# Routed experts in groups of 512 tokens instead of tiles of 128, turned by VectorE

## The chip, the cores and the metric

The kernel runs on one core of one Trainium2 chip, in one launch. The metric is the time on the device in microseconds; the median of three runs stands for a kernel. The five engines go by the profile's short names: PE (TensorE; PEld its weight loads), DVE (VectorE), ACT (ScalarE), POOL (GpSimd) and SP (SyncE, which here only issues DMAs).

## The reference

x is 8 blocks of 512 tokens of 512 numbers. Two layers are added to it. The first is a matrix for each block, made by a small network from the block's condition. The second, which this change is about, has a shared part and routed experts (8 of them, each token at its top 2):

```python
shared = jax.nn.silu(xf @ w1) * (xf @ w3) @ w2           # 512 -> 1024 -> 512
s = jax.nn.sigmoid((jnp.concatenate([xf, tf], axis=-1) @ router_W).astype(jnp.float32))
sel_scores = s + router_bias
_, topk_idx = jax.lax.top_k(sel_scores, K)               # K = 2
s_sel = jnp.take_along_axis(s, topk_idx, axis=1)
denom = s_sel.sum(axis=1, keepdims=True)
gates = jnp.where(denom > 1e-09, s_sel / (denom + 1e-09), 1.0 / K).astype(x.dtype)
combine = jnp.zeros((N, E), x.dtype).at[jnp.arange(N)[:, None], topk_idx].add(gates)
h = jax.nn.gelu(jnp.einsum('nc,ech->enh', xf, W1e), approximate=False)
y = jnp.einsum('enh,ehc->enc', h, W2e)
routed = jnp.einsum('ne,enc->nc', combine, y)
return ((shared + routed) / (N_SHARED + K)).reshape(Bb, Tt, C)   # added to x
```

The kernel computes y only for the experts that a token has chosen.

## The kernel before, in words

Every product is done in float32r in three matmuls (helper `mm3`): each operand is cut into a high part (a cast by ACT, or by POOL for expert weights) and a low part (a subtraction by DVE, or POOL), and high x high, high x low and low x high are accumulated in PSUM. A matmul has a stationary side of 128 x 128 and a moving side of 512 columns.

The order of the work is written out by hand for each engine, with semaphores. The stages:

1. The first layer (to about 233 us), block by block. It leaves x1 three times: turned for the products (`x1T_d`), in token order (`x1_d`, stored from `x1tok`), and each token's row twice in `xs_d`, at a place in the region of each of its experts. POOL writes those by indirect DMA (L701) from `x1tok`, which ACT fills from PSUM (`keep_tok`, L802).
2. The shared FFN of block 7 (`ffn(S, ...)`, L1676): 8 chunks of the hidden width, each with 24 matmuls up (into `K` and `L` or `Rb`) and 12 down (into `M[0..3]`). For a chunk, ACT does silu (L445), DVE the product (L458), ACT the high part `gTh` (L448), DVE the low part `gTl` (L460); what is in `after` is done behind a chunk. Behind chunk 3, DVE makes the table of the tiles (`tables`, L941): a chain of small steps, each waiting for the last. SP writes it to DRAM and reads it back into one partition (`tab_i`); then each engine reads its numbers from it with `value` and uses them as addresses. SP puts 128 rows of zeros behind each expert's rows (L577) and zeros into the end of `ys_d` (L569).
3. The experts, tile by tile of 128 rows, two tiles in a loop pass (`rpair`). For a tile, SP loads the rows (L588), PE turns them with four transposes (`tx`, L1660), ACT and DVE cut them (L897, L1276); the first product (`mm1`, 12 matmuls into `L`) has the rows as stationary side and the expert's W1 as moving side; ACT applies gelu (L901); PE turns the result (`th`, L1703), ACT and DVE cut it (L905, L1281); the second product (`mm2`, 12 matmuls into `Rb`) follows, DVE evicts it (L1297), SP stores it to `ys_d` (L604). PE's order is mm1(t+1), tx(t+2), mm2(t), th(t+1). The weights are cut by POOL, once for an expert, into one of two halves of `weh` and `wel` (L722 to L728), and PE picks the half by a register.
4. The FFN of blocks 0 to 6 (`fblock`), seven times 288 matmuls, in a loop. Beside it the sum of a block: x1 in token order is loaded into `xres`, DVE adds the shared part from `M` (L1316, frees `M` for the next block) and the two gathered expert rows times their gates (L1324; POOL gathers them from `ys_d`, L752). SP stores `xres` and only then loads the next.

Of the kernel before, what the change touches and what calls it, by code (L numbers as in the profile page):

```python
# [5 lines left out]
ALU = mybir.AluOpType  # L6
ACT = mybir.ActivationFunctionType
F32 = mybir.dt.float32
# [12 lines left out]
ROW, WOFF, WCNT, AROW, FREE, PAD, PAIRS, NACT = range(8)  # L21

def build(nc, x, cond, base, cw1, cb1, cw2, cb2, ln_g, ln_b, rw, rb, w1, w3, w2, w1e, w2e, out):
# [9 lines left out]
    REGION = N + P  # L34
    ROWS = E * REGION + P
    WSL = KC * HE
# [3 lines left out]
    TILES = (N * TOPK + E * (P - 1)) // P  # L40
    PAIRS_MAX = (TILES + 1) // 2
    TAB = -(-(TILES + 5) // 8) * 8
# [21 lines left out]
    xs_d = nc.dram_tensor("xs_d", (ROWS, D), F32, kind="Internal").ap()  # L64
    tab_d = nc.dram_tensor("tab_d", (TAB, 8), I32, kind="Internal").ap()
    ys_d = nc.dram_tensor("ys_d", (PAIRS_MAX * 2 * P, D), F32, kind="Internal").ap()

# [14 lines left out]
    with ExitStack() as ctx:  # L82
# [12 lines left out]
        TX, TH, HP, YP = K[0], K[1], L, Rb  # L95
# [48 lines left out]
        tabi = sb("tabi", [P, 8], I32)  # L144
        tab = sb("tab", [P, 8])
# [23 lines left out]
        tab_i = sb("tab_i", [1, TAB * 8], I32)  # L169
        sb("route_hold", [P, 160])  # L170
# [5 lines left out]
        with ExitStack() as st:  # L176
            xgh = sb("xgh", [P, KC, P], F32R, st)
            xgl = sb("xgl", [P, KC, P], F32R, st)
            hTh = sb("hTh", [P, KC, P], F32R, st)
            hTl = sb("hTl", [P, KC, P], F32R, st)  # L180
            hg = sb("hg", [P, HE], F32, st)
            yo = sb("yo", [P, 2, D], F32, st)
# [4 lines left out]
        with ExitStack() as st:  # L187
# [7 lines left out]
            zz = sb("zz", [P, GT, 32], F32, st)  # L195
        slf = sb("slf", [P, 2, T])
# [26 lines left out]
        with ExitStack() as st:  # L223
            weraw = sb("weraw", [P, WSL], F32, st)
            xr = sb("xr", [P, 2, D], F32, st)
            weh = sb("weh", [P, 2, 2 * WSL], F32R, st)
            wel = sb("wel", [P, 2, 2 * WSL], F32R, st)
        with ExitStack() as st:
            x1raw = sb("x1raw", [P, KC * T], F32, st)
            xres = sb("xres", [P, TT, D], F32, st)  # L230
            yb = sb("yb", [P, TT * TOPK, D], F32, st)
# [62 lines left out]
        scat = [sem(f"scat{i}") for i in range(6)]  # L294
        tabs = sem("tabs")
        dt_ = sem("dt")
        dy = sem("dy")
        pad_out = sem("pad_out")
# [16 lines left out]
        xr_in = [sem(f"xr_in{i}") for i in range(2)]  # L315
        xg_ps = sem("xg_ps")
# [94 lines left out]
        def tiles(eng, pairs, body):  # L411

            body(0)
            with eng.Fori(1, pairs) as j:
                body(j)
# [1344 lines left out]
```

## Time and profile before

| | us |
|---|---|
| median of 3 runs | 1199.97 (1197.99 to 1203.39) |
| the profiled execution | 1202.75 |
| its span in the trace | 1200.9 |
| mean granted TensorE clock | 0.985 of full |

The profile is of one execution; its span begins with the first instruction and ends with the last. Where PE's matmuls overlap, the distance between two starts says what one costs, not its duration. `L1375` is line 1375 of the kernel; L1375 to L1377 are the three matmuls of `mm3`. The buffers' numbers are left out, so that K is either of two banks.

### The profile page before, as it was taken

The page shows a single profiled execution, that of the slowest core. Times are in us where ns is not written, and L with a number is a line of the kernel's source. Part 1 is how long each engine was busy: PE and PEld are TensorE (multiplying, and loading weights), DVE is VectorE, ACT ScalarE, POOL GpSimd, SP SyncE. Part 2 cuts the span into 40 slices and gives each one's busy share as a digit, 9 for nine tenths or more (in the row PEclk, how much of TensorE's full clock was granted, in tenths as well). Part 3 has the DMA queues.
Part 4 walks back from the last instruction along what each step waited for, and adds up shares of the span by engine and source line. Part 5 has one row for each costly group of instructions (what it writes and reads, how often), then busy time and mean ns, then how long its engine had stood idle before and what let it go on. Part 6 is the DMA issues. An engine that isn't in the chain of part 4 may idle for free.

```text
span 1200.9 us, 18241 instructions
## 1 busy us (share of the span) xinstructions
PE 1160.2 (97%) x5762; PEld 935.4 (78%) x5763; DVE 416.4 (35%) x812; ACT 287.8 (24%) x498; POOL 188.1 (16%) x207
## 2 busy tenths in 40 slices
PE   6999898899999999999999998999999999999998
PEld 5666676778788888888888887888888888888887
DVE  4104653535233333333333334233333314233334
ACT  2212453521222222222222222121211112121211
POOL 2002165642510000000000003202020010202020
PEclk8999999899999999999999999999999999999999
DMA  8562589895332222222222224404031130404031
GB/s 309 227 239 95 207 299 347 289 306 162 129 118 83 79 87 79 79 87 79 82 84 83 83 79 123 175 1 175 1 100 74 39 136 0 175 0 175 0 125 49
DMA packets 70480, 151.82 MB, mean 126 GB/s; under 512 B 9753, under 2 KB 18457, under 8 KB 68658
## 3 DMA queue, kind: packets, MB, share of 16 engines
q1 hardware_dynamic: 57666, 111.55, 26.9%
q0 software_dynamic: 12784, 39.86, 9.4%
q8 instruction: 20, 0.33, 0.1%
q14 instruction: 10, 0.08, 0.0%
HBM read 88.73 MB, written 62.65 MB: 126 GB/s over the span
## 4 chain that ended last, share of the span: by engine, by line
PE 91%; DVE 4%; DMA 2%; POOL 1%; issue 1%; ACT 1%; SPq 0%; DVEq 0%; ACTq 0%
PE L L1375 7%; PE L L1377 7%; PE L L1376 7%; PE Rb L1377 7%; PE Rb L1375 7%; PE Rb L1376 7%; PE M L1375 5%; PE M L1376 5%; PE M L1377 5%; PE K L1376 5%; PE K L1375 5%; PE K L1377 5%; PE Rb L1465 3%; PE K L1703 2%; PE K L1660 2%; PE M L1403 2%
## 5 line engine op out<-in xcount | busy, mean ns | idle before, releaser
L752 POOL DMA_INDIRECT yb<-ys_d,pos_fix x64 | 61.2, 957 | 326.6 <-DVE xres L1324 308.6
L1375 PE MATMUL L<-weh,xgh 128*128 x260 | 107.6, 414 | 1.8 <-issue 1.8
L1276 DVE TENSOR_TENSOR xgl<-K,xgh 128x512 fp32r<-128x512 f32 x66 | 45.7, 692 | 173.4 <-ACT xgh L897 173.4
L1375 PE MATMUL Rb<-weh,hTh 128*128 x256 | 105.5, 412 | 0.0
L1375 PE MATMUL K<-x1h,w13h 128*128 128x512 f32 x256 | 101.6, 397 | 3.0 <-DVE x1l L1355 3.0
L1375 PE MATMUL M<-w2h,gTh 128*128 128x512 f32 x256 | 102.3, 399 | 2.3 <-DVE gTl L460 2.3
L1377 PE MATMUL L<-weh,xgl 128*128 x260 | 102.7, 395 | 0.0
L1376 PE MATMUL L<-wel,xgh 128*128 x260 | 102.5, 394 | 0.0
L1376 PE MATMUL K<-x1l,w13h 128*128 128x512 f32 x256 | 102.0, 398 | 0.0
L1376 PE MATMUL M<-w2l,gTh 128*128 128x512 f32 x256 | 101.9, 398 | 0.0
L1377 PE MATMUL M<-w2h,gTl 128*128 128x512 f32 x256 | 101.8, 398 | 0.0
L1377 PE MATMUL K<-x1h,w13l 128*128 128x512 f32 x256 | 101.7, 397 | 0.0
L1377 PE MATMUL Rb<-weh,hTl 128*128 x256 | 100.5, 393 | 0.0
L1376 PE MATMUL Rb<-wel,hTh 128*128 x256 | 100.2, 391 | 0.0
L445 ACT ACTIVATE slf<-K 128x512 f32<-128x512 f32 x64 | 38.3, 599 | 238.3 <-PE K L1377 234.2
L448 ACT CAST gTh<-slf 128x512 fp32r<-128x512 f32 x64 | 39.7, 621 | 191.7 <-DVE slf L458 191.7
L458 DVE TENSOR_TENSOR slf<-L,slf 128x512 f32<-128x512 f32 x32 | 22.1, 692 | 169.2 <-PE L L1377 162.5
L905 ACT CAST hTh<-K 128x512 fp32r<-128x512 f32 x65 | 38.2, 587 | 163.9 <-PE K L1703 163.9
L1297 DVE COPY yo<-Rb 128x512 f32<-128x512 f32 x64 | 44.3, 692 | 92.2 <-PE Rb L1377 92.2
L701 POOL DMA_INDIRECT xs_d<-x1tok,pos_int x64 | 68.2, 1065 | 38.0 <-issue 24.6
L901 ACT ACTIVATE hg<-L 128x512 f32<-128x512 f32 x65 | 38.9, 598 | 146.5 <-PE L L1377 146.5
L746 POOL COPY pos_fix<-ypos 128x8 int32 (+1 forms) x8 | 2.3, 283 | 442.6 <-DMA ys_d<-yo 390.0
(238 smaller groups left out, 2146.1 us busy)
## 6 DMA issues: line engine op xcount, KB each, us to landing
xr<-xs_d SPq DMA_DIRECT2D x68, 256.0 KB, 2.6
w2c<-in_L_cond_w_dram SPq DMA_DIRECT2D x8, 2048.0 KB, 8.5
ys_d<-yo SPq DMA_DIRECT2D x64, 256.0 KB, 2.1
xtok<-in_x_dram SPq DMA_DIRECT2D x32, 256.0 KB, 7.4
x_d<-x1tok SPq DMA_DIRECT2D x8, 1024.0 KB, 7.9
xres<-x_d SPq DMA_DIRECT2D x8, 1024.0 KB, 9.5
x1T_d<-xp SPq DMA_DIRECT2D x7, 1024.0 KB, 4.6
out_dram<-xres SPq DMA_DIRECT2D x7, 1024.0 KB, 4.8
```

Of the source, the lines that this page charges most:

```text
L445: nc.scalar.activation(slf[:, h % 2], U[h % 2][:], ACT.Silu).then_inc(ffn.silu, 1)
L448: nc.scalar.copy(gTh[:, h % 2], slf[:, h % 2]).then_inc(ffn.g_hi, 1)
L701: pool.indirect_dma_start(out=xs_d, out_offset=bass.IndirectOffsetOnAxis(ap=pos_int[:, c:c + 1].bitcast(U32), axis=0), in_=x1tok[i][:, t, ...
L752: pool.indirect_dma_start(out=yb[:, c, :], out_offset=None, in_=ys_d, in_offset=bass.IndirectOffsetOnAxis(ap=pos_fix[:, c:c + 1].bitcast(U ...
L901: nc.scalar.activation(hg[:], HP[:], ACT.Gelu).then_inc(h_g, 1)
L905: nc.scalar.copy(hTh[:].rearrange("p k n -> p (k n)"), TH[:]).then_inc(ht_hi, 1)
L1276: tt(xgl[:].rearrange("p k n -> p (k n)"), TX[:], xgh[:].rearrange("p k n -> p (k n)").bitcast(F32), ALU.subtract).then_inc(xg_lo, 1)
L1297: nc.vector.tensor_copy(yo[:, s], YP[:]).then_inc(y_sb, 1)
L1375: mm(o, ah, bh_, start=start, stop=False)
L1376: mm(o, ah, bl_, start=False, stop=False)
L1377: return mm(o, al, bh_, start=False, stop=stop)
L1465: last_mm = mm(Rb[32 * q:32 * q + 32, cc * P:(cc + 1) * P], hTz[:, k, 2 * j + part], w[:, k, 2 * q + j], start=(n == 0 and j == 0 and k == 0),
```

## The change

The experts are worked in groups of 512 rows instead of tiles of 128. A region of `xs_d` now ends in 512 rows of padding, the table has 4 columns instead of 8 (`ROW`, `EROW`, `PAD`, `LAST`), and a group knows its expert's rows in W1e and W2e.

- For each group the whole weights are loaded by SP (`load_e1`, `load_e2`), even if the expert is that of the last group, and cut by ACT and DVE in four pieces each. POOL cuts no weights.
- The rows come by four DMAs that place them so that 32 x 32 blocks turned by DVE (`turn_rows`) give x turned; the columns of `x1tok`, `x1_d` and `xs_d` are permuted for that, and DVE undoes it in the first sum of each tile (`fused`, four instructions instead of one).
- The first product has W1 as stationary side and the 512 tokens as moving side, so h comes out turned; no transpose by PE is left in this stage. The second goes chunk by chunk of h over all four token tiles, into the four banks `G`.
- ACT evicts y into `yo`, SP stores it in two halves. The sum goes into `total` instead of into `xres`.
- The zeros: 8 DMAs of 512 rows into `xs_d` from SP, ahead of the load of the first weights, and 7 of 512 rows into `ys_d` from POOL after it.
- x1 of block 0 is loaded and cut in the last group, between evictions.

The core of the diff:

```diff
+        G = K + V
+            sp.wait_ge(tab_in, 16)
+            pad_src = zeros[:].unsqueeze(1).broadcast_to([P, GR * D // (P * P), P])
             with sp.Fori(0, E) as e:
-                row = value(sp, PAD, e, E * REGION - P)
-                sp.dma_start(zero_rows(row), zero_src).then_inc(pad_out, 16)
+                row = value(sp, PAD, e, E * REGION - GR)
+                sp.dma_start(xs_d[ds(row, GR), :].rearrange("(p r) (k c) -> p (r k) c", p=P, c=P), pad_src).then_inc(pad_out, 16)
...
+            def load_rows(g):
+                row = value(sp, ROW, g, E * REGION - GR)
+                rows = xs_d[ds(row, GR), :].rearrange("(n t) (j f) -> j t n f", t=32, j=4)
+                for j in range(4):
+                    sp.dma_start(xr[32 * j:32 * j + 32].rearrange("p t i f -> p (t i) f"), rows[j]).then_inc(xr_in, 16)
...
+            load_e1(0)
+            sp.wait_ge(pad_out, 16 * E)
+            load_rows(0)
+            load_e2(0)
+
+            def load_group(g, n):
+                if n is not None:
+                    sp.wait_ge(e1_lo, n * KC)
+                    load_e1(n)
+                    sp.wait_ge(xt_f, n * TT)
+                    load_rows(n)
+                    sp.wait_ge(e2_lo, n * KC)
+                    load_e2(n)
...
+                sp.wait_ge(ys_zero, 16 * (GROUPS_MAX - SURE))
+                store_y(g, 0)
+                store_y(g, 1)
...
+            pool.wait_ge(e1_in, 16)
+            for g in range(SURE, GROUPS_MAX):
+                pool.dma_start(ys_d[g * GR:(g + 1) * GR, :].rearrange("(p r) (k c) -> p (r k) c", p=P, c=P), zero_src
+                               ).then_inc(ys_zero, 16)
...
+            after[HC - 2] = lambda: [cut_e1(0, m) for m in range(KC)]      # ACT, and the same on DVE
+            ffn_act(act, S, 0, True, after)
+            act.sem_inc(y_sb, Y_FREE)
+            for t in range(TT):
+                cut_x(0, t)
+            def pass_group(g, n):                                          # ACT
+                cut_e2(g, 0)
+                cut_e2(g, 1)
+                gelu(g, 0)
+                cut_e2(g, 2)
+                gelu(g, 1)
+                cut_e2(g, 3)
+                if n is not None:
+                    cut_e1(n, 0)
+                gelu(g, 2)
+                if n is not None:
+                    cut_e1(n, 1)
+                gelu(g, 3)
+                if n is not None:
+                    cut_x(n, 0)
+                    cut_e1(n, 2)
+                    cut_x(n, 1)
+                    cut_e1(n, 3)
+                    cut_x(n, 2)
+                    cut_x(n, 3)
+                keep_y(g, 0)
+                keep_y(g, 1)
+                if n is None:
+                    act.wait_ge(x1raw_in, 16)
+                    act.wait_ge(h_ps, g * KC + KC)
+                    cut_x1(0)
+                keep_y(g, 2)
+                keep_y(g, 3)
...
+            def turn_rows(g, t):
+                dve.wait_ge(xr_in, g * 64 + 64)
+                if not (first(g) and t < 2):
+                    dve.wait_ge(xg_lo, g * TT + (t - 1))
+                nc.vector.transpose(xt[:, t % 2].rearrange("p c (i n) -> p i c n", i=4),
+                                    xr[:, t].rearrange("p i (c f) -> p i c f", c=KC)).then_inc(xt_f, 1)
+            def pass_group(g, n):                                          # DVE
+                cut_e2(g, 0)
+                cut_e2(g, 1)
+                cut_h(g, 0)
+                cut_e2(g, 2)
+                cut_h(g, 1)
+                cut_e2(g, 3)
+                if n is not None:
+                    turn_rows(n, 0)
+                    cut_e1(n, 0)
+                cut_h(g, 2)
+                if n is not None:
+                    turn_rows(n, 1)
+                    cut_e1(n, 1)
+                cut_h(g, 3)
+                if n is not None:
+                    cut_x(n, 0)
+                    cut_e1(n, 2)
+                    turn_rows(n, 2)
+                    cut_x(n, 1)
+                    cut_e1(n, 3)
+                    turn_rows(n, 3)
+                    cut_x(n, 2)
+                    cut_x(n, 3)
...
+            def mm1(g):
+                pe.wait_ge(xg_lo, g * TT + TT)
+                for m in range(KC):
+                    pe.wait_ge(e1_lo, g * KC + m + 1)
+                    pe.wait_ge(y_sb, g * TT + (m - TT + 1 + Y_FREE))
+                    cols = slice(m * P, (m + 1) * P)
+                    for k in range(KC):
+                        last_mm = mm3(G[m][:], e1h[:, k, cols], e1l[:, k, cols], x1h[:, k], x1l[:, k], k == 0, k == KC - 1)
+                    last_mm.then_inc(h_ps, 1)
+
+            def mm2(g):
+                for m in range(KC):
+                    pe.wait_ge(ht_lo, g * KC + (m + 1 + H_FREE))
+                    pe.wait_ge(e2_lo, g * KC + m + 1)
+                    for t in range(TT):
+                        if m == 0:
+                            pe.wait_ge(h_g, g * KC + t + 1)
+                        rows = slice(t * P, (t + 1) * P)
+                        last_mm = mm3(G[t][:], hTh[:, m, rows], hTl[:, m, rows], e2h[:, m], e2l[:, m], m == 0, m == KC - 1)
+                        if m == KC - 1:
+                            last_mm.then_inc(y_ps, 1)
```

## Rows read from the trace of the kernel before

**Rows 1.** The page's busy times: us (share of the span) x instructions:

```profile
PE 1160.2 (97%) x5762; PEld 935.4 (78%) x5763; DVE 416.4 (35%) x812; ACT 287.8 (24%) x498; POOL 188.1 (16%) x207
```

**Rows 2.** Busy time by stage: us, each engine's busy (x), PEclk, DMA share, GB/s:

```profile
233.60:305.50 71.90, 69.60 (x294) 55.44 (x293) 33.05 (x90) 19.24 (x28) 33.44 (x26) 0.98 0.71 236
305.50:311.80 6.30, 4.22 (x22) 3.17 (x21) 1.38 (x2) 1.66 (x3) 2.52 (x2) 1.00 0.31 95
311.80:722.14 410.34, 410.34 (x2047) 340.03 (x2048) 131.45 (x191) 105.77 (x191) 14.33 (x6) 1.00 0.26 88
722.14:725.50 3.36, 0.37 (x4) 0.13 (x3) 2.16 (x4) 2.04 (x4) 0.00 (x0) 1.00 0.29 103
725.50:1197.40 471.90, 471.87 (x2016) 379.24 (x2016) 156.03 (x242) 82.83 (x139) 63.48 (x72) 1.00 0.24 82
726.00:728.80 2.80, 2.80 (x8) 2.22 (x7) 1.29 (x3) 1.50 (x2) 1.62 (x3) 0.50 0.87 311
```

**Rows 3.** Chain of waits, 700 to 740 us: start, us, what:

```profile
702.91 0.44 PE K L1703 x4
725.53 0.58 PE K L1375
726.53 0.43 PE K L1377
```

**Rows 4.** Groups by form: count | busy us, mean ns | idle before:

```profile
L1375 PE MATMUL L<-weh,xgh 128*128 x260 | 107.6, 414 | 1.8 <-issue 1.8
L1375 PE MATMUL Rb<-weh,hTh 128*128 x256 | 105.5, 412 | 0.0
L1660 PE MATMUL K<-ident,xr 128*128 128x128 f32 x264 | 39.4, 271 | 0.0
L1703 PE MATMUL K<-ident,hg 128*128 128x128 f32 x260 | 38.9, 272 | 0.3 <-ACT hg L901 0.3
```

**Rows 5.** Timeline of PE in the experts: start, us, engine, line:

```profile
403.25 0.39 PE L1376 MATMUL L<-wel,xgh 128*128 x1
405.77 0.60 PE L1660 MATMUL K<-ident,xr 128*128 128x128 f32 x4
```

**Rows 6.** Timeline of PE in an FFN block:

```profile
799.95 0.40 PE L1375 MATMUL K<-x1h,w13h 128*128 128x512 f32 x1
805.55 0.40 PE L1375 MATMUL M<-w2h,gTh 128*128 128x512 f32 x1
```

**Rows 7.** Timeline of DVE and SP's queue, and one window of zero writes:

```profile
267.80 0.16 DVE L956 SCALAR_TENSOR_TENSOR tw<-iota,taken 128x8 f32<-128x8 f32 x1
274.87 0.35 SPq L571 DMA_DIRECT2D tab_d<-tabi  x1
278.78 14.04 SPq L577 DMA_DIRECT2D xs_d<-zeros  x8
268.00:269.00 1.00, 1.00 (x6) 0.82 (x5) 0.86 (x5) 0.00 (x0) 0.00 (x0) 1.00 1.00 288
```

**Rows 8.** DMA issues: count, KB each, median us from issue to landing:

```profile
weraw<-in_L_cond_W1e_dram POOLq DMA_DIRECT2D x2, 1024.0 KB, 6.0
x1raw<-x1T_d SPq DMA_DIRECT2D x6, 1024.0 KB, 12.7
```

**Rows 9.** Groups by form of DVE and ACT, columns as in group 4:

```profile
L1165 DVE STREAM_TRANSPOSE zz<-L 32x128 f32<-32x128 f32 x32 | 10.0, 313 | 0.6
L1276 DVE TENSOR_TENSOR xgl<-K,xgh 128x512 fp32r<-128x512 f32 x66 | 45.7, 692 | 173.4 <-ACT xgh L897 173.4
L934 ACT CAST x1h<-x1raw 128x512 fp32r<-128x512 f32 x28 | 15.2, 615 | 0.9 <-DVE hTl L1281 0.9
```

**Rows 10.** Timelines of ACT and DVE at two places:

```profile
296.54 0.60 ACT L445 ACTIVATE slf<-K 128x512 f32<-128x512 f32 x1 [4.16 <-PE K L1377]
300.79 1.99 DVE L460 TENSOR_TENSOR gTl<-slf,gTh 128x512 fp32r<-128x512 f32 x1 [0.69 <-ACT gTh L448]
800.22 0.69 DVE L458 TENSOR_TENSOR slf<-L,slf 128x512 f32<-128x512 f32 x1 [3.93 <-PE L L1377]
```

More of the change, by code:

```diff
@@ L408, in value, with groups @@
             alone(eng)
-            return eng.value_load(tab_i[0:1, ds(at_ * 8 + col, 1)], min_val=lo, max_val=hi)
[L411 to L415, printed above, removed]
+            return eng.value_load(tab_i[0:1, ds(at_ * COLS + col, 1)], min_val=lo, max_val=hi)
+        H_FREE, Y_FREE, YO_FREE = 2, KC, 16
+        def groups(eng, body):
+            last = value(eng, LAST, 0, GROUPS_MAX - 1, 1)
+            with eng.Fori(0, last) as g:
+                body(g, g + 1)
+            body(last, None)
+            return last
         def alone(eng):
@@ new lines, in keep_y, with cut_x1 @@
+            def keep_y(g, t):
+                act.wait_ge(y_ps, g * TT + (t + 1 + Y_FREE))
+                act.wait_ge(y_out[t // 2], g * 16 + YO_FREE)
+                nc.scalar.copy(yo[:, t], G[t][:]).then_inc(y_sb, 1)
+            def cut_x1(b):
+                for c in range(KC):
+                    nc.scalar.copy(x1h[:, c], x1raw[:, c * T:(c + 1) * T]).then_inc(xf_hi, 1)
+            after = {h: lambda h=h: cut_piece(UP_PIECES + 1 + h) for h in range(PIECES - UP_PIECES - 1)}
+            after[HC - 2] = lambda: [cut_e1(0, m) for m in range(KC)]
@@ L1306, in prepare, with fused @@
                 dve.wait_ge(xres_in, m * 16 + 16)
+                if not first(m):
+                    dve.wait_ge(out_st, m * 16)
+            def fused(t, part, scale, n, done_):
+                if n is not None:
+                    dve.wait_ge(acc, n)
+                    ins = nc.vector.scalar_tensor_tensor(out=total[:, t], in0=part, scalar=scale, in1=total[:, t],
+                                                         op0=ALU.mult, op1=ALU.add)
+                else:
+                    for j in range(4):
+                        ins = nc.vector.scalar_tensor_tensor(
+                            out=total[:, t].rearrange("p (c j f) -> p j c f", j=4, c=KC)[:, j],
+                            in0=part.rearrange("p (c j f) -> p j c f", j=4, c=KC)[:, j], scalar=scale,
+                            in1=xres[:, t].rearrange("p (j c f) -> p j c f", j=4, c=KC)[:, j],
+                            op0=ALU.mult, op1=ALU.add)
+                ins.then_inc(done_, 1)
             def add_shared(t, of, n, done_):
@@ L1726, in fblock, with pass_group, banks_f @@
+            pe.sem_inc(y_ps, Y_FREE)
+            pe.wait_ge(tab_in, 16)
+            pe.wait_ge(S.silu, HC)
+            pe.wait_ge(S.g_f, HC)
+            def pass_group(g, n):
+                mm1(g)
+                mm2(g)
+            last = groups(pe, pass_group)
+            def banks_f(h, i):
+                t = G.index((U, V)[i][h])
+                pe.wait_ge(y_sb, last * TT + (t + 1 + Y_FREE))
             def fblock(b):
-                ffn(F, b, (lambda h, i: None) if first(b) else None, lambda k: pe.wait_ge(xf_lo, b * KC + k + 1),
+                ffn(F, b, banks_f if first(b) else None, lambda k: pe.wait_ge(xf_lo, b * KC + k + 1),
```

395 lines of the change are left out of this document (145 added, 250 removed).

## The prediction

> **What bounds the kernel now.** First the page's busy shares [rows 1]: TensorE is busy for 97% of the span, no other engine over 35%. So a change pays only where it takes work from TensorE, or where TensorE stands still. Then the table by stage [rows 2]: the experts run from 305.50 to 722.14 us (416.6 us), with TensorE without a gap from 311.80; ahead of them is a start with some 2 us idle, behind them 3.4 us of which it works 0.4, then 471.9 us of seven FFN blocks, 67.41 each. The chain of waits [rows 3] shows what fills the experts: matmuls, and between them groups of four transposes at 0.44 us a group; and at the change of stage a restart in which matmuls take 0.43 us each instead of some 0.23, the granted clock being 0.50, the lower level (1.2 GHz) [rows 2], after an idle of 3 us. Eight or so such matmuls cost 1.6 us.
>
> How many tiles: the first expert product has 65 x 4 matmuls of each of its three kinds, the second 64 x 4 [rows 4]. And W1e is loaded from DRAM only twice [rows 8], once for an expert that has rows: two experts are in use. 4096 tokens, each at two different experts, in 64 tiles of 128: both have 4096 rows, 32 full tiles. In groups of 512 that is 16 full groups, none padded, and one expert's weights serve eight groups.
>
> **The matmuls.** Before, 64 tiles x 24 = 1536 matmuls of 512 columns; after, 16 x (48 + 48) = 1536. The same number (the extra 65th first product, 2.7 us, goes). Between 403.25 and 405.77 lie 11 dynamically addressed matmuls, 0.2291 each [rows 5]; between 799.95 and 805.55 lie 24 of the FFN with fixed addresses, 0.2333 each [rows 6]. After the change every operand of the experts has a fixed address and the form of the FFN (128 columns cut from a 512-wide tile against a whole 512 chunk). I take 0.2333: 1536 x 0.2333 = 358.4 us. The other end, 0.2291, gives 351.9. 
>
> **The transposes.** 264 + 260 of them [rows 4], 131 groups at 0.44 = 57.6 us, all on TensorE's path. They go: rows of x come by DMA as 32-partition bands and VectorE turns them in 32x32 blocks, and h comes out turned since the weights are now the stationary side. A tile was 24 x 0.2291 + 2 x 0.44 = 6.38 us, which times 64 is 408.6; the new 22.4 us a group times 16 is 358.4.
>
> **What ACT and DVE get for it, per group of 22.4 us.** ACT: 4 casts each of e2, e1, x and h, 4 gelus, 4 evictions of y: 24 at 0.615 at most [rows 9] = 14.8. DVE: 16 subtractions at 0.69 [rows 9] = 11.0, and four turns of 128x512. A turn of 32x128 takes 0.313 [rows 9]; for 512 elements the ends are 0.313 and 4 x 0.313 = 1.25; I take 0.75, near the 0.69 of the other 512-element operations. 14.0 together. Both fit, so order and arrival count:
> - First product 0 to 11.2 us of the group, its four chunks at 2.8 apiece; second 11.2 to 22.4, y chunks ready at 20.3, 21.0, 21.7, 22.4.
> - ACT: casts of e2 from 0.7, gelu(0) at 2.9, gelu(1) 5.7, gelu(2) 8.5, gelu(3) 11.3 to 11.9. The second product's first chunk overwrites the bank of tile 3 at 13.3: 1.4 us to spare.
> - SP is in order: store y (0.8), load e1 of the next group, its rows (four DMAs), e2. A loop pass with a table read and an issue takes SP 14.04 / 8 = 1.8 us [rows 7]. e1 is issued at 2.6 and lands at 8.6 (6.0 for 1 MB [rows 8]), wanted from 7.6; the rows come behind it, 1 MB at 288 GB/s [rows 7] = 3.6 us: 12.2.
> - From there DVE works off four turns, four subtractions of e1, two of h, four of x: 4 x 0.75 + 10 x 0.62 (back to back) = 9.2, ending at 21.4. The next group needs all of x at 22.4. One us of slack, the tightest place of the steady state.
> Loop overhead: an FFN block takes 67.41 against 288 x 0.2333 = 67.19, so 0.2 a pass, 15 passes: 3.0 us.
>
> **The start, where the change pays.** The padding of xs_d grows from 9 x 256 KB to 8 x 1 MB = 8.39 MB, and now stands in SP's queue ahead of the load of e1; ACT and DVE cut e1 ahead of the last chunk of the shared FFN, and x rows wait for all padding. The table is made in 16 short linked steps instead of 33 from 267.80 (0.21 each): the store goes out at 271.2, not 274.87; padding starts 3.9 later, as before (274.87 to 278.78) [rows 7], at 275.1, data from 277. Zero writes alone ran at 288 GB/s with the DMA engines full [rows 7]: 29.1 us, to 306.2. e1 behind it: cast possible from 310.2. ACT then casts e1 (2.4), and only then does silu(7), at 312.7 instead of 296.54 [rows 10]; slf(7), gTh(7), gTl(7) follow, and TensorE's last chunk of the shared FFN, which could have started at 302, starts at 315.6: 13.6 us idle. It ends at 320.0, slow restart included. The rows of group 0 have landed at some 313.4; DVE's four turns and four subtractions from 315.5 end at 320.9. First expert matmul at 321.0 instead of 305.50 (first product of tile 0). What gets better here: POOL no longer cuts weights, beside which gTl(7) took 1.99 instead of 0.69 [rows 10].
> Bounds of this start: with padding at twice the speed (landed by 292) nothing waits but x itself, and TensorE starts the experts at 307; with padding at half the speed, 350.
> POOL writes another 7.3 MB of zeros into ys_d from 311, and SP waits for these ahead of the first store of y, with the load of e1(2) queued behind. All that is to move after 306 (7.3 MB of zeros, 2.1 of rows, 3.1 of weights) takes 41 us, to 347, while the first store of y is due at 343: the rows of group 2 are late by some 3 us against a slack of 1, part of which the queue makes good. I put 1.5 us, once (0 to 6).
>
> The Trainium skill (DMA: Bandwidth & Descriptors, Queues, rings and completion order) says that each DMA engine goes round between the queues that have work, packet by packet. The trace has no place to show it for a zero write beside a load. By it e2(0), e1(1) and the rows of group 1 get half the engines each time, and the latter land at 334 instead of 320; DVE would then cut h(2) at 336, wanted at 338. It changes no term, but eats the cover.
>
> **The end.** Before: last tile, cast of h, x1 cut after it, restart at half clock, 725.53 [rows 3]. Now x1 of block 0 is loaded in group 15 and cut between evictions of y, at 21.7 of the group: first k at 23.0, 0.7 us gap, no 3 us idle. Gain against before: 2.7 of gap, 1.6 of restart.
> **The FFN blocks.** Adding into a total splits each first sum in four (16 x 0.31 at most instead of 4 x 0.62: 2.5 us more for DVE ahead of the block's first slf, before which it stands idle for 3.93 [rows 10]): nothing; in the last block it sits before slf(7), 0.7 us. Casts of x1tok in a permuted order: same number of elements, nothing.
>
> **The sum.** 321.0 + 358.4 + 3.0 + 1.5 + 0.7 = 684.6, where block 0 starts now at 725.53. Then 1200.9 - 725.53 - 1.6 + 0.7 = 474.5. Span 1159.1 against 1200.9: 41.8 us less. The profiled execution took 1202.75, 1.85 over its span; so 1161 on its scale. The median shown is 1199.97; less 41.8 that is 1158. I predict 1159.
>
> **Rivals.**
> - Matmuls at 0.2291 as in the old experts: 1152. For: it was so in this stage for 400 us. Against: all fixed-address stages show 0.2333.
> - Rows of the next group late, or the turn at 1.25 us: 1 to 2 us idle in each of 15 groups, 1174 to 1189. For: the slack is 1 us by my own count, built from bounds. Against: SP's time of 1.8 for a pass is from a DMA-bound stretch.
> - Padding slower than 288 GB/s, at half: 29 us more at the start, 1188. Against: 288 was measured in three windows of 1 us on end, one of which is shown.
> - Slower than before: the loads of a group take what x1raw takes in the FFN blocks, 12.7 us [rows 8]. e1 then lands at 15.3, gelu(2) stalls the second product, rows land near 19, x is ready at 28, 5.6 us late; with 1.6 for the restart at the lower clock 7 a group, 108 in all: 1266. It decides where the stall passes 41.8 / 15 = 2.8 us a group. Against: those loads run beside the gathers of yb, which the experts don't have.
> - It doesn't do what it says: more than 16 groups, if experts were more than two. Excluded by the two loads.
>
> **Chances.** Forecast 0.54, the matmul rate 0.16, late rows or slow turns 0.17, slow padding 0.08, slower loads 0.04, anything near no change 0.01. The likeliest one's own range is 1153 to 1168; with the matmul rate below, and most of the late rows above, 1148 to 1182. Faster by over 0.5% (what can be told from no change here) 0.95, same 0.01, slower 0.04.
>
> **What would show it.** No transposes between 320 and 684; TensorE's idle of 12 to 15 us around 302 to 316, ended by DVE's gTl, with ACT waiting on the e1 DMA; then some 22.4 to 22.6 us a group at full granted clock; spacing 0.2333; block 0 a us after the last y. Wrong: a regular gap at each group's start ended by DVE's x1l (late rows), a turn near 1.25, no idle at 302, or groups at 22.0.

## The result, and the profile after

The changed kernel takes 1181.8 us in the median of 4 runs (1181.18 to 1184.73), against 1200.96 for the kernel before in 4 runs (1197.99 to 1203.39; three of them are those of the first table): a ratio of 0.9846, 95% interval 0.9818 to 0.9875. A second time, with 5 runs beside 17 of before, it was 1180.94 and 0.9863 (0.9842 to 0.9883). So it is faster, by some 19 us (1.5%), where 42 were forecast. 1181.8 lies just inside the end of the range, and only since errors of opposite sign met, as shown below. The profiled execution took 1181.49, its span is 1179.5.

The page's busy shares (us, share of the span, instructions) already say that something stands in the way:

```profile
PE 1096.6 (93%) x5226; PEld 878.3 (74%) x5226; DVE 482.2 (41%) x1015; ACT 393.8 (33%) x687; POOL 164.3 (14%) x200
```

TensorE was at 97% [rows 1]; now its work is 64 us less and 83 us of the span are idle. The table by stage (columns as in rows 2) places the idle. The stages are: shared FFN, its last chunk with the wait for x, group 0, group 1, groups 2 to 15, FFN blocks; then two short windows used below.

```profile
233.60:309.48 75.88, 58.73 (x254) 47.00 (x252) 25.21 (x65) 15.70 (x24) 21.13 (x21) 0.93 0.80 241
309.48:315.72 6.24, 4.42 (x12) 3.25 (x13) 5.26 (x8) 3.40 (x5) 3.16 (x3) 0.76 1.04 395
315.72:352.84 37.12, 26.20 (x96) 20.94 (x97) 12.45 (x20) 13.69 (x25) 0.00 (x0) 0.77 0.77 238
352.84:377.55 24.71, 22.21 (x97) 17.78 (x96) 12.45 (x20) 13.17 (x25) 0.00 (x0) 1.00 0.61 170
377.55:710.36 332.81, 312.45 (x1344) 250.16 (x1345) 167.97 (x270) 184.28 (x332) 0.00 (x0) 1.00 0.63 174
710.36:1179.50 469.14, 465.58 (x2016) 378.52 (x2016) 163.76 (x339) 83.79 (x141) 62.53 (x72) 1.00 0.24 85
337.00:343.00 6.00, 0.00 (x0) 0.00 (x0) 0.12 (x1) 0.00 (x0) 0.00 (x0) 0.50 1.01 179
386.00:391.00 5.00, 5.00 (x23) 4.13 (x23) 0.00 (x0) 3.38 (x6) 0.00 (x0) 1.00 1.24 197
```

Groups 2 to 15 take 332.81 / 14 = 23.77 us each, where 22.6 were forecast; group 0 takes 37.12; the FFN blocks 469.14 instead of 474.5. TensorE's waits of the whole kernel, the three longest (engine, tile and line that waited, then whose release came last: us in total, times, longest):

```profile
PE M L1445 <- DVE gTl L475: 17.5, 3, 14.5
PE K L1445 <- ACT yo L930: 17.3, 14, 1.3
PE K L1445 <- DVE hTl L1318: 15.4, 8, 10.9
```

The first is the start that was forecast. The second comes 14 times, once for each of groups 2 to 15: a regular gap. The third is one stall of 10.9 in group 0 and seven small ones. VectorE's own waits say what is behind the last two (count | busy us, mean ns | idle before, and what ended it). Under it stand rows of the first and of the second expert product:

```profile
L1298 DVE STREAM_TRANSPOSE xt<-xr 128x512 f32<-128x512 f32 x64 | 45.0, 705 | 111.2 <-DMA xr<-xs_d 111.0
L1445 PE MATMUL K<-x1h,e1h 128*128 128x512 f32 x128 | 51.7, 404 | 19.1 <-ACT yo L930 17.3 <-DVE x1l L1304 1.8
L1445 PE MATMUL K<-e2h,hTh 128*128 128x512 f32 x128 | 52.1, 407 | 15.8 <-DVE hTl L1318 15.4
```

VectorE stood idle for 111.0 us before its turns, waiting for rows of x: 7 us a group. A turn takes 705 ns.

**One group, read closely.** The timeline from 377.55, where TensorE starts a group (start, us, engine, line, idle before):

```profile
377.80 1.38 SPq L613 DMA_DIRECT2D ys_d<-yo  x2
381.08 0.40 SPq L597 DMA_DIRECT2D e1raw<-in_L_cond_W1e_dram  x1
382.41 2.02 SPq L608 DMA_DIRECT2D xr<-xs_d  x4
392.20 0.71 DVE L1298 STREAM_TRANSPOSE xt<-xr 128x512 f32<-128x512 f32 x1 [6.33 <-DMA xr<-xs_d]
398.80 0.71 DVE L1298 STREAM_TRANSPOSE xt<-xr 128x512 f32<-128x512 f32 x1
399.49 0.39 PE L1447 MATMUL Rb<-e2h,hTl 128*128 128x512 f32 x1
399.54 0.62 ACT L917 CAST x1h<-xt 128x512 fp32r<-128x512 f32 x1 [1.18 <-DVE xt L1298]
400.07 1.07 ACT L930 COPY yo<-K 128x512 f32<-128x512 f32 x2
401.13 0.47 PE L1445 MATMUL K<-x1h,e1h 128*128 128x512 f32 x1 [1.25 <-ACT yo L930]
```

SP issues e1 at 3.5 us of the group (2.6 forecast), since both stores of y stand ahead of it in its queue, each waiting for ScalarE's evictions. The rows follow at 4.9 and are there at 14.65 (12.2 forecast), not 3.6 but 5.6 us behind e1: the window 386 to 391 above, in which the rows travel and e2 is issued behind them, shows 197 GB/s at a DMA share of 1.24, not the 288 of the zero writes [rows 7]. The last turn starts at 21.25, the cast of it follows, and only behind this cast in ScalarE's order come the evictions of y that free the banks. TensorE has finished at 399.7 and starts at 401.13. The profile names ScalarE's eviction; but that eviction, and the last subtraction of x as well, stand behind VectorE's turn, and the turns behind the rows. Experiments 1 and 2 test that.

**Group 0** shows the same thing larger:

```profile
315.13 10.37 SPq L608 DMA_DIRECT2D xr<-xs_d  x4
342.88 0.71 DVE L1298 STREAM_TRANSPOSE xt<-xr 128x512 f32<-128x512 f32 x1 [17.25 <-DMA xr<-xs_d]
344.82 0.79 PE L1445 MATMUL K<-e2h,hTh 128*128 128x512 f32 x1 [10.92 <-DVE hTl L1318]
```

The rows of group 1 are wanted while POOL's 7.3 MB of zeros are under way: four DMA issues keep SP for 10.4 us, the rows are there 27.7 us after the first of them, and VectorE, which stands at the first turn, has the cut of h(2) queued behind it. So TensorE stops in the middle of the second product, and restarts on the lower level of the clock (0.50 in the window 337 to 343; behind 344.82 a matmul takes 0.43 us, as in rows 3).

### The profile page after: what moved, and what is told of

It reads as the page before. It is cut to its first block, busy times and chain, and to the rows that moved or that the text cites. A ratio compares the mean times of both kernels' runs of the same rounds, so it can differ in the third digit from the quotient of the medians.

```text
span 1179.5 us, 15385 instructions
## 1 busy us (share of the span) xinstructions
PE 1096.6 (93%) x5226; PEld 878.3 (74%) x5226; DVE 482.2 (41%) x1015; ACT 393.8 (33%) x687; POOL 164.3 (14%) x200
## 4 chain that ended last, share of the span: by engine, by line
PE 55%; DMA 15%; DVE 12%; SPq 7%; issue 7%; ACT 2%; POOL 1%; ACTq 0%; DVEq 0%; POOLq 0%
DMA xr<-xs_d 12%; PE K L1445 5%; PE K L1447 5%; PE K L1446 5%; PE M L1445 4%; PE M L1446 4%; PE M L1447 4%; SPq L419 3%; DVE xt L1298 3%; PE Rb L1535 3%; PE L L1447 2%; PE L L1446 2%; PE L L1445 2%; PE Rb L1447 2%; PE Rb L1446 2%
## 5 line engine op out<-in xcount | busy, mean ns | idle before, releaser
L1298 DVE STREAM_TRANSPOSE xt<-xr 128x512 f32<-128x512 f32 x64 | 45.0, 705 | 111.2 <-DMA xr<-xs_d 111.0
L917 ACT CAST x1h<-xt 128x512 fp32r<-128x512 f32 x64 | 39.7, 621 | 115.3 <-DVE xt L1298 115.3
L728 POOL DMA_INDIRECT xs_d<-x1tok,pos_int x64 | 67.2, 1050 | 34.4 <-issue 18.6
L1445 PEld LDWEIGHTS M<-w2h,gTh 128*128 128x128 f32 x256 | 48.5, 189 | 30.3 <-DVE gTl L475 18.8
L1445 PE MATMUL K<-x1h,e1h 128*128 128x512 f32 x128 | 51.7, 404 | 19.1 <-ACT yo L930 17.3
L473 DVE TENSOR_TENSOR slf<-Rb,slf 128x512 f32<-128x512 f32 x32 | 22.1, 691 | 114.0 <-PE Rb L1447 114.0
L1445 PE MATMUL K<-e2h,hTh 128*128 128x512 f32 x128 | 52.1, 407 | 15.8 <-DVE hTl L1318 15.4
L1318 DVE TENSOR_TENSOR hTl<-hg,hTh 128x512 fp32r<-128x512 f32 x64 | 43.9, 686 | 52.2 <-ACT hTh L925 52.2
L475 DVE TENSOR_TENSOR gTl<-slf,gTh 128x512 fp32r<-128x512 f32 x64 | 44.3, 692 | 47.5 <-ACT gTh L463 47.5
L1473 PE MATMUL M<-xTh,bh 128*128 128x512 f32 x128 | 56.2, 439 | 6.0 <-DVE bl L1129 3.2
L1447 PEld LDWEIGHTS M<-w2h,gTl 128*128 128x128 f32 x256 | 48.4, 189 | 11.7
```

The source lines that it names most:

```text
L473: nc.vector.tensor_tensor(slf[:, h % 2], V[h % 2][:], slf[:, h % 2], ALU.mult).then_inc(ffn.g_f, 1)
L475: nc.vector.tensor_tensor(gTl[:, h % 2], slf[:, h % 2], gTh[:, h % 2].bitcast(F32), ALU.subtract).then_inc(ffn.g_lo, 1)
L728: pool.indirect_dma_start(out=xs_d, out_offset=bass.IndirectOffsetOnAxis(ap=pos_int[:, c:c + 1].bitcast(U32), axis=0), in_=x1tok[i][:, t, ...
L917: nc.scalar.copy(x1h[:, :, t * P:(t + 1) * P], xt[:, t % 2]).then_inc(xg_hi, 1)
L1298: nc.vector.transpose(xt[:, t % 2].rearrange("p c (i n) -> p i c n", i=4), xr[:, t].rearrange("p i (c f) -> p i c f", c=KC)).then_inc(xt_f, 1)
L1318: tt(hTl[:, m], hg[:, m % 2], hTh[:, m].bitcast(F32), ALU.subtract).then_inc(ht_lo, 1)
```

## The experiments

Experiments 1 to 4 were run side by side, so were 5 to 8, and so were the second run of 1 with 9 and 10; 11 had only the kernel before beside it. Up to the store of the tables an execution can take up to 22 us longer than in the changed kernel's first profile; for the kernel before it is 7 to 9 us (experiment 10). It isn't the chip alone: experiments 1 to 4 and 5 to 8 ran on the same one, and the kernel before took 1212.49 beside the first four and 1198.35 beside the others. What moves this stage is not known. So what an edit does is read from the stages behind that store, and times are compared within one such set of runs.

**1. Stores of y from ScalarE's queue.** Edit, in SP's and in ScalarE's order of work:

```diff
-                store_y(g, 0)      # SP, at the end of load_group
-                store_y(g, 1)
+                store_y(g, 0)      # ScalarE, behind keep_y(g, 1)
+                store_y(g, 1)      # ScalarE, behind keep_y(g, 3)
```

The wait for the zeros in `ys_d` goes with the stores.

> The stores of y are issued from ACT's queue behind its evictions, so that SP doesn't wait for them ahead of the next group's loads; all else as in the changed kernel. Theory A (the groups wait for the rows of the next one, which land 14.6 us into a group because SP issues their loads only after the last store of y): SP issues e1 some 5 us earlier, the rows land near 9.5, the gap of 1.4 us at each group's start is gone; 1181.8 less 14 x 1.4 = about 1162. Rival B (what comes last is the serial work of DVE and ACT on a group, whatever the arrival): the gap stays, 1180 to 1184.

Measured: 1176.26 (1169.26 to 1181.19), ratio to before 0.9683 (0.9602 to 0.9764), tables stored at 286.06 instead of 264.30. It was run a second time beside experiment 9, in which the changed kernel's own stages are unaltered:

> The stores of y from ScalarE's queue once more, on a chip where the tables of the changed kernel come at 264 and not at 286. Theory A (the late rows of groups 2 to 15 are their whole excess): 14 x 2.0 us less than the changed kernel's 1180.9, 1153 to 1156, all groups from 1 on at 21.76. Theory B (its 1176 of the first run was no accident of the chip): 1170 or more.

Measured: 1169.19 (1167.81 to 1175.06), ratio 0.9675 (0.9634 to 0.9716), against 1197.94 for the kernel of experiment 9: 28.8 us less, where 14 x 2.0 = 28 were expected. The tables came at 279.61 here and at 278.48 there, so the expectation's condition of tables at 264 wasn't met, and its absolute figure isn't tested. The windows of group 0, of groups 1 to 15, and of one group, and VectorE's turns with their wait for rows:

```profile
332.46:368.80 36.34, 24.48 (x97) 19.69 (x97) 12.45 (x20) 13.22 (x24) 0.00 (x0) 0.81 0.80 245
368.80:695.20 326.40, 326.40 (x1441) 270.17 (x1439) 180.67 (x288) 199.41 (x352) 0.00 (x0) 1.00 0.66 189
390.56:412.32 21.76, 21.76 (x98) 18.02 (x96) 12.45 (x20) 13.58 (x24) 0.00 (x0) 1.00 0.66 215
L1298 DVE STREAM_TRANSPOSE xt<-xr 128x512 f32<-128x512 f32 x64 | 44.9, 703 | 23.2 <-DMA xr<-xs_d 23.0
```

PE busy equals the window: 326.40 / 15 = 21.76 a group without one gap, in both runs. VectorE's wait for rows falls from 111.0 us to 23.0, of which 18.2 is the stall of group 0, which stays. 21.76 / 96 is 0.2267 us a matmul, below both ends that I had taken. So the regular gap goes when the two stores no longer stand in front of the loads, and theory A holds. Stage by stage, the two profiles differ by 27.9: groups 2 to 15 with the turn to block 0 take 306.3 instead of 334.5 (28.2 less), group 1 takes 1.7 less, and all else together is 2.0 longer. The absolute expectations (1162; 1153 to 1156) were missed, as the early stage was 15 to 22 us longer than in the first profile.

**2. Rows as 2 KB pieces.** The rows load unsplit, four DMAs of 128 whole rows. This kernel leaves out the order of x that the turns need, so it serves for the time alone. Two things change at once: the size of a piece, and the partitions that a DMA fills, 128 instead of 32.

```diff
-                rows = xs_d[ds(row, GR), :].rearrange("(n t) (j f) -> j t n f", t=32, j=4)
+                rows = xs_d[ds(row, GR), :].rearrange("(j p) d -> j p d", p=P)
                 for j in range(4):
-                    sp.dma_start(xr[32 * j:32 * j + 32].rearrange("p t i f -> p (t i) f"), rows[j]).then_inc(xr_in, 16)
+                    sp.dma_start(xr[:, j].rearrange("p i f -> p (i f)"), rows[j]).then_inc(xr_in, 16)
```

> The rows of a group are read as whole rows of 2 KB instead of four pieces of 512 B each; x then stands in another order, so what is turned isn't the x of the reference, all times of the engines being the same. Theory A with the size of the piece as its cause (1 MB of rows at some 190 GB/s, 5.6 us, where whole rows of weights come at some 380): rows land 2.8 us earlier, gap gone, and group 0 gains as well: 1155 to 1162. If the order in SP's queue alone makes them late: rows still land past 13 us, 1175 or more. Rival B: 1180 to 1184.

Measured: 1158.86 (1155.01 to 1163.42), ratio 0.9536 (0.9466 to 0.9606). In one group, which starts at 493.17:

```profile
496.42 0.40 SPq L597 DMA_DIRECT2D e1raw<-in_L_cond_W1e_dram  x1
504.75 0.71 DVE L1298 STREAM_TRANSPOSE xt<-xr 128x512 f32<-128x512 f32 x1 [3.35 <-DMA xr<-xs_d]
```

SP's order is unchanged and e1 goes out at 3.25, yet the first turn is at 11.6, 3.1 earlier than in the changed kernel, and every group from 1 on takes 21.76. Between 498.0 and 503.5 the DMA engines moved 352 GB/s at a share of 0.98, against 261 at 1.16 in the like stretch of the changed kernel (383.5 to 392). Group 0 lasts 28.35, its stall is 3.4. So the form of the rows' DMAs is a second cause; whether it is the size of a piece or the 32 partitions isn't separated. Either cure alone removes the gap of groups 2 to 15: the two delays add up on one chain, whose excess is 2 us a group.

**3. Padding of 128 rows.**

```diff
-                sp.dma_start(xs_d[ds(row, GR), :]..., pad_src).then_inc(pad_out, 16)
+                sp.dma_start(xs_d[ds(row, P), :].rearrange("p (k c) -> p k c", c=P), pad_src[:, 0:KC]).then_inc(pad_out, 16)
```

> Padding of xs_d is 128 rows an expert instead of 512 (here no row of it is ever read, all groups being full): 2.1 MB instead of 8.4 ahead of the first weights. Theory: TensorE's idle from 294.9 to 309.5 goes, first expert matmul at about 302 instead of 315.7 (-14), and since POOL's zeros into ys_d then start at 280 and not at 304, the stall of 11.3 us in group 0 goes too (-13): about 1155. Rival (the stall in group 0 comes from the loads' own size): only -14, about 1168.

Measured: 1184.41 (1180.16 to 1189.47), ratio 0.9766 (0.9689 to 0.9843), tables at 279.85. SP's padding and TensorE's two waits of the start:

```profile
284.81 14.91 SPq L586 DMA_DIRECT2D xs_d<-zeros  x8
312.62 0.51 PE L1445 MATMUL M<-w2h,gTh 128*128 128x512 f32 x1 [2.10 <-DVE gTl L475]
318.92 0.77 PE L1445 MATMUL K<-x1h,e1h 128*128 128x512 f32 x1 [3.24 <-DVE x1l L1304]
```

14.91 instead of 24.91 for a quarter of the bytes, at a DMA share of 0.42: what is left is SP's loop, 1.86 a pass. From the store of the tables to the first expert matmul it is 39.1 us, 51.4 in the changed kernel: 12.3 saved, 14 expected. The stall of group 0 stays, 11.0, as the rival had it; but POOL's zeros went out only at 307.70, behind the load of e1, and not at 280, so this experiment doesn't tell whether the zeros cause it. The next one does.

**4. Zeros into ys_d early.** POOL issues the seven zero writes ahead of its wait for XW (66.26 us) instead of at 304.56.

```diff
+            pool.wait_ge(cond_ps, 4)
+            for g in range(SURE, GROUPS_MAX):
+                pool.dma_start(ys_d[g * GR:(g + 1) * GR, :]..., zero_src).then_inc(ys_zero, 16)
             pool.wait_ge(xw_hi, 1)
...
-            pool.wait_ge(e1_in, 16)
```

> The 7 MB of zeros into ys_d are issued by POOL near 65 us, where the DMA engines are half busy, instead of at 304. Theory: the idle at 295 to 309 stays, the stall of 11.3 us in group 0 and its restart go: about 1168. Rival (the rows of group 1 are late by the loads alone): 1178 or more. If the early zeros delay the loads of the first stage, that stage is longer by up to 5 us.

Measured: 1188.18 (1185.15 to 1189.68), ratio 0.9792 (0.9722 to 0.9862), tables at 279.42. Groups 0 and 1:

```profile
331.25:353.09 21.84, 21.84 (x97) 18.09 (x97) 12.55 (x20) 13.51 (x25) 0.00 (x0) 1.00 0.42 97
353.09:376.58 23.49, 22.25 (x97) 17.78 (x96) 12.46 (x20) 13.07 (x25) 0.00 (x0) 1.00 0.67 179
```

45.3 instead of 61.8: 16.5 less, and no stall. The later groups keep their gap. So the stall was these zeros. The time itself gives 1188 where 1168 was expected: the tables came 15 us later than in the first profile, and the FFN blocks were at the longer of their two lengths (experiment 9).

**5 and 6. The changed and the first kernel again,** on one chip, as controls.

> The changed kernel once more, as the control for the others on this chip. Groups 2 to 15 at 23.8 us each with an idle of 1.25 ahead of each, group 0 with a stall of 11 us: these come from the kernel and return. The store of the tables was at 264.3 us in its first profile and at 279 to 286 in the four experiments run on another chip. Theory A: this early stage is bound by transfers and moves with chip and execution, so it is at 270 to 286 here, and the ratio to the kernel before stays at 0.98 to 0.99 since that one has the same stage. Theory B: the 6.9 us by which the early stage was shorter than before's (274.87 less the 3.7 of the shorter table) is the change's: the store stays within 2 us of 264.

> The kernel before, with a profile on the same chip. By A its tables are stored as much later than 274.87 as the changed kernel's are later than 264.3, within 5 us; by B the difference between the two is again 10 to 11 us, and more than the 3.7 of the shorter table in every pair. The FFN blocks: 67.4 us each as before if the length belongs to the program; the changed kernel had 67.0 in two profiles and 67.4 in three, so I expect it to vary by some 0.4 with no cause in the code.

Measured: 1180.94 (1179.16 to 1183.76), ratio 0.9863; and 1197.33 (1194.49 to 1202.58), ratio 0.9994 (0.9976 to 1.0013). The stores of the tables, before and after:

```profile
273.33 0.35 SPq L571 DMA_DIRECT2D tab_d<-tabi  x1
```

```profile
263.34 0.32 SPq L577 DMA_DIRECT2D tab_d<-tabi  x1
```

10.0 us between them, as 10.6 the first time. In other sets the changed kernel's store moves by more than that (A), but here the difference stays 6.3 above the 3.7 of the shorter table (B). All of the changed kernel's gaps return: an idle of 1.25 ahead of 14 groups, 12.1 in group 0.

**7 and 8. The three edits together, and the tables earlier.** Experiments 1, 3 and 4 in one kernel; then besides it

```diff
-            after[3] = lambda: tables(dve)
+            piece1 = after[1]
+            after[1] = lambda: [piece1(), tables(dve)]
...
+            after[HC - 2] = lambda: [[cut_e1(0, m) for m in range(KC)], dve.wait_ge(tab_in, 16),
+                                     turn_rows(0, 0), turn_rows(0, 1)]
...
-            dve.wait_ge(tab_in, 16)
-            turn_rows(0, 0)
-            turn_rows(0, 1)
```

> Stores of y from ScalarE's queue, zeros into ys_d written at some 65 us, padding of 128 rows, together. Theory A (three separate waits, each with its own cause): tables to first expert matmul 39 us as with the short padding alone (51.4 in the changed kernel), group 0 without its stall, all 16 groups at 21.76: 280 + 39 + 348 + 2 to block 0, 470 behind it, 1139 of span, 1141 in time; ratio to the changed kernel 0.952 to 0.962. Theory B (the rows' 512-byte pieces at some 188 GB/s are the bound, and what one edit frees another takes): 5 to 20 us above that, with DVE waiting for rows in most groups.

> The same with the tables made after chunk 1 of the shared FFN instead of chunk 3, and the first two turns of group 0 ahead of VectorE's last chunk. Theory A: tables are stored 15 us earlier, padding, e1 and rows of group 0 are there before the shared FFN ends, TensorE never waits at 302 and for 1 to 3 us ahead of the first expert matmul: 5 us less than with the three edits alone, 1136. Theory B: VectorE then waits for rows inside its chunk 7 or the tables' data come late, and it is the same or 3 us more.

Measured, beside the two controls: 1123.55 (1120.26 to 1127.02), ratio to before 0.9374 (0.9355 to 0.9394), and 1120.58 (1113.35 to 1121.36), ratio 0.9339 (0.9313 to 0.9364). Against the changed kernel's 1180.94 that is 57.4 and 60.4 less. The first one's windows from the last shared chunk on (that chunk and the wait for x, group 0, groups 1 to 15):

```profile
294.67:301.83 7.16, 3.06 (x12) 2.20 (x13) 5.26 (x8) 3.40 (x5) 0.00 (x0) 1.00 0.77 269
301.83:325.30 23.47, 23.47 (x97) 19.23 (x97) 12.54 (x20) 13.03 (x24) 0.00 (x0) 0.93 0.51 139
325.30:651.70 326.40, 326.40 (x1441) 270.09 (x1439) 180.83 (x288) 199.32 (x352) 0.00 (x0) 1.00 0.67 186
```

The single gains add up: 28.8 (stores) + 12.3 (padding) + 16.5 (zeros) = 57.6, against 57.4. That they agree to 0.2 is luck: the changed kernel's groups 2 to 15 alone took 332.8 and 336.0 in two profiles. From the store of the tables to block 0 the kernel of the three edits is 57.8 us shorter than the changed kernel beside it, and its FFN blocks are 2.5 longer in all. All groups from 1 on are at 21.76, so nothing that one edit freed was taken by another, and theory A holds; the ratio to the changed kernel is 0.951, where 0.952 to 0.962 was expected. The absolute times lie 15 to 18 us under the expectation, since the tables came at 262.74 and 250.60 and not at 280 and 265. Of the second, the start and all sixteen groups:

```profile
297.87 0.47 PE L1444 MATMUL K<-x1h,e1h 128*128 128x512 f32 x1 [1.02 <-DVE x1l L1304]
```

```profile
297.87:646.03 348.16, 348.16 (x1536) 288.18 (x1536) 193.38 (x308) 212.51 (x376) 0.00 (x0) 1.00 0.67 184
```

The experts are 1536 matmuls without a gap, and start 4.0 us earlier (5 expected); the times alone (intervals that overlap) would not show that. The tables were stored 12.1 us earlier, but from there to the experts it takes 47.3 us instead of 39.1: all but 1.0 of the two waits of the start is gone, and TensorE has no more to gain there. This one is the fastest kernel of the study.

**9. Where TensorE's program lies.** Five semaphore increments on TensorE's queue ahead of the shared FFN.

```diff
+            for _ in range(5):
+                pe.sem_inc(spare, 1)
```

> The changed kernel with five semaphore increments more on TensorE's queue ahead of the shared FFN, which do nothing else. An FFN block took 67.20 us in both profiles of before, 66.44 in three (the changed kernel twice, the short padding) and 66.7 to 66.8 on the mean in the others, to 0.02 the same within each kernel, while TensorE's instructions and its operands' places are the same in all but before. Theory A: the length hangs on where TensorE's loop lies in the program, which every other edit shifts too: blocks of some other length, 66.6 to 67.3, here. Theory B: it comes from the work on the other queues (it was the edits to stores and zeros that changed it): 66.44 again. Groups 2 to 15 at 23.8 and 1181 to 1186 by both.

Measured: 1197.94 (1193.01 to 1201.88), ratio 0.9892 (0.9857 to 0.9927), tables at 278.48. One FFN block each (us, busy) of the kernel before, of the changed one, of experiment 7, and of this one:

```profile
794.36:861.56 67.20, 67.20 (x290) 54.03 (x289) 21.29 (x34) 11.84 (x20) 7.77 (x9) 1.00 0.22 79
```

```profile
776.88:843.32 66.44, 66.44 (x289) 54.10 (x288) 22.04 (x46) 11.84 (x20) 7.80 (x9) 1.00 0.22 79
```

```profile
720.13:787.05 66.92, 66.92 (x290) 54.20 (x289) 22.05 (x47) 11.84 (x20) 7.78 (x9) 1.00 0.22 79
```

```profile
791.21:857.65 66.44, 66.44 (x290) 54.10 (x288) 22.05 (x47) 11.84 (x20) 7.78 (x9) 1.00 0.22 79
```

66.44 is what theory B expected, but B falls as well: the kernel of experiment 1 had 66.8 in its first profile and 66.44 in its second, with not a byte changed. The length varies from one execution to another, 66.44 or 66.8 to 66.9, in kernels after; in three profiles of kernels before (experiment 10 among them) it was 67.2. What sets it stays open.

**10. The regions of xs_d.** The kernel before with `REGION = N + 4 * P` instead of `N + P`, as after.

> The kernel before with 4608 rows of xs_d to an expert instead of 4224, as the changed kernel has it, and nothing else. Its tables were stored at 274.87 and 273.33, the changed kernel's at 264.30 and 263.34; 3.7 of the 10.3 is the shorter table. Theory A: the other 6.6 comes from where the scatter writes its rows in DRAM: store at 267 to 269 here, and 4 to 7 us less in time. Theory B: from something else (the place of the program, the zeros written to ys_d at 255 us): store at 273 to 275, time as before.

Measured: 1212.47 (1208.39 to 1219.44), ratio 1.0019 (0.9995 to 1.0043), tables at 281.88, where those of experiment 9's kernel beside it came at 278.48. The place of the rows in DRAM gains nothing in time. In this set the difference between the two kernels is 3.4, the shorter table and no more; so the 6.3 to 6.9 of the sets with early tables isn't a fixed property of the change either.

**11. Full padding with the early tables.** Experiment 8 with 512 rows of padding again.

> The kernel of the early tables with the full padding back (512 rows to an expert), for the question whether the 10 us of it matter once the tables come early. From the store of the tables it takes 4.6 to the first padding, 24.9 for the padding, 3.4 and 8.1 to e1 in SBUF, 41.0 in all, and rows of group 0 some 2 us later. With the early tables that store was 45.9 us ahead of TensorE's last chunk of the shared FFN having its operand (296.5 at its end less 250.6). Theory A: e1 lands 2 to 5 us ahead of the need and the first expert matmul is 3 to 6 us later than with the short padding: 1123 to 1127 on a chip with tables at 250, a ratio to the kernel before of 0.937 to 0.941. Theory B: the padding's queue holds back the last pieces of the shared weights, which are still being loaded at 250, and silu(7) waits again: 10 us or more, 0.945 or above.

Measured: 1154.65 (1153.0 to 1155.96), ratio 0.9499 (0.9471 to 0.9528), tables at 271.86. The stretch from the store of the tables to their coming back, the wait for e1, and TensorE's wait that follows from it:

```profile
271.86:277.40 5.54, 5.54 (x25) 4.52 (x25) 0.74 (x2) 0.63 (x2) 1.92 (x2) 1.00 1.03 407
316.88 2.18 ACT L895 CAST e1h<-e1raw 128x512 fp32r<-128x512 f32 x4 [11.95 <-DMA e1raw<-in_L_cond_W1e_dram]
326.02 0.79 PE L1444 MATMUL M<-w2h,gTh 128*128 128x512 f32 x1 [11.38 <-DVE gTl L475]
```

Theory A failed. The numbers are those of B (10 us or more, 0.945 or above), its mechanism is not: e1 landed 45.0 us after the store, not 41.0, because from the store to the first padding it took 8.4 us, not 4.6. The tables now travel while the DMA engines are full (share 1.03) with the store of x1 and POOL's last scatters. Experiment 8 had shown it (250.60 to 258.82), and I left it out. TensorE reached its wait 42.8 us behind the store, so e1 was late for silu(7), which stands behind the cast of e1, as in the changed kernel. From tables to experts it is 59.4 us, 47.3 with the short padding: 12.2, as in experiment 3 (12.3). The difference of the two ratios, 0.016 or 19 us, is larger; the rest lies ahead of the store of the tables, before the padding is written, where sets differ without a known cause.

## Why the prediction was wrong, point by point

| | forecast | measured | difference |
|---|---|---|---|
| store of the tables | 271.2 | 264.30 | -6.9 |
| from there to the first expert matmul | 49.8 | 51.4 | +1.6 |
| groups 0 and 1 | 46.7 | 61.8 | +15.1 |
| groups 2 to 15 and the turn to block 0 | 316.9 | 332.8 | +15.9 |
| FFN blocks | 474.5 | 469.1 | -5.4 |
| span | 1159.1 | 1179.5 | +20.4 |

- **Number of groups, no transposes, work per group:** right. 16 groups of 96 matmuls. ACT works 184.28 / 14 = 13.2 and DVE 12.0 a group, 14.8 and 14.0 were put.
- **Matmul rate:** 0.2333 was taken, with 0.2291 as the other end; it is 0.2267 in the experts (experiments 1, 2, 7, 8), and a pass of the loop costs nothing to be seen. That is 10.2 + 3.0 = 13.2 us too dear, which hid a part of the other error. Going by likeness to the FFN's form was no ground: neither form predicted the rate. The Trainium skill (TensorE: Matmul & The Clock Gate, Wait — 56ns, not 53.3ns?) has 2.5 ns over N / 2.4 GHz, so 215.8 ns; even the best stretch lies 11 ns above it.
- **The failed step: "One us of slack, the tightest place of the steady state", from e1 "issued at 2.6", "1 MB at 288 GB/s" and "22.4 us".** Measured: e1 issued at 3.5 and landed at 9.1 (+0.5 against 8.6), rows 5.6 behind it (+2.0 against 3.6), so at 14.65 for 12.2; VectorE's chain 8.7 instead of 9.2; and the group is to last 21.76, not 22.4. So x is ready at 23.35 where it was wanted at 21.76. What this costs is 332.8 - 14 x 21.76 - 0.7 = 27.5 us over groups 2 to 15; 28.2 came back there, against experiment 9's kernel, when the stores left SP's queue (experiment 1). The table shows only 15.9 for them, since the matmul rate and the passes gave 12 back: so the time stayed inside the range by luck. The rate of the rows was the weakest term: 288 GB/s was read off writes of a constant tile and used for reads in 512-byte pieces.
- The Trainium skill (DMA: Bandwidth & Descriptors, Specifications) puts the full rate at 512 bytes and above. These runs differ, as far as experiment 2 tells: 512-byte reads of xr into 32 partitions gave 261 GB/s together with e1, 2 KB ones into 128 partitions 352.
- **The rival "rows of the next group late"** was this mechanism, priced at 1 to 2 a group and 1174 to 1189; 2.0 a group and 1181.8 were measured. It was held for less likely than the forecast, 0.17 against 0.54; the slack of 1 us was built from three terms each uncertain by 1, and should have had the larger share.
- **Zeros into ys_d, the second step that failed:** 1.5 (0 to 6) was put, 15.3 in group 0 and 1.2 in group 1 is what they cost (experiment 4 gives back 16.5). The sum behind the 1.5 has a slip too: 12.5 MB at 288 GB/s is 43 us, not 41. I let the rows of group 2 be late, against the first store. They were late for group 1 already, since the zeros were under way at the same time; the prediction's paragraph on the sharing between queues had named this (rows at 334). It changed "no term" there only because the rows of group 1 were held to be wanted after h(2); in VectorE's order the turn stands ahead of it, and they landed at 342.8.
- **The start:** an idle of 13.6 forecast, 14.5 measured, at the forecast place and with ACT waiting 19.04 us for e1. Zero writes ran at 284 GB/s from 271 to 293. Experiment 3 shows that 12 us from the tables to the experts are the size of the padding; that SP's loop makes the rest wasn't tested.
- **The end:** 0.7 us gap forecast, 0.66 idle measured at 710.36, and no restart at the lower clock.
- **The transposes:** 64 tiles of 6.38 us are 408.2, not 408.6; nothing hangs on it.
- **FFN blocks:** "nothing" was wrong by 5.3: 66.44 a block against 67.20. **Tables:** 6.9 earlier than 271.2. Neither was in the forecast as anything but zero, both came in its favour, and neither is explained (experiments 9 and 10 excluded a cause each).

## What to carry to other kernels

In a loop where one queue both stores results and loads the next inputs, every load waits for the last result: put the stores on another queue before counting on any slack (here 28.8 us of 1198). The wait that the profile names for it can be two engines away from the cause, so follow it back through what each engine has queued. A transfer's rate is to be taken from a transfer of the same direction and piece size, and fill-in writes of zeros belong where the DMA engines have room (here near 66 us), since an engine that waits for one late load holds back all that is queued behind it. When the slack in a steady loop is smaller than the sum of the errors of its terms, take the late case for the likelier one; it is paid in every pass.

## What the runs showed that I had not expected

- Matmuls of 512 columns, at the full granted clock and without a wait, start 0.2267 us apart in the experts and 66.44 / 288 = 0.2307 or 67.20 / 288 = 0.2333 apart in FFN blocks; the same program showed 66.44 and 66.8 in two executions.
- DMAs of 256 KB in a loop of SP cost 1.86 us a pass at a DMA share of 0.42; and four issues of 256 KB took 10.4 us when the DMA engines had 7.3 MB of another queue to work off.
- A wait named after ScalarE's eviction (17.3 us in total) came from the rows: it went with the stores' move to another queue, though ScalarE then issued the stores on top of the same work.
